# A recurrent block and an FP4 gated block on one core: the loop over two chunks written out as sixteen chunks

## The reference

```python
xn = layernorm(x)
# attention branch
a  = causal_dwconv3(rmsnorm(xn)) @ pw.T + b + xn          # x1
hidden, gate = split(rmsnorm(a) @ gru_w.T)                # 256 + 256
h[t] = sigmoid(-gate[t]) * h[t-1] + sigmoid(gate[t]) * g(hidden[t])
b_ = h + a                                                # x2
s  = gelu(rmsnorm(b_) @ w1.T + b1) @ w2.T + b2 + b_       # 256 -> 1024 -> 256
# gated branch, inputs and weights rounded to FP4 in blocks of 16
q  = fp4(xn)
hid = silu(q @ fp4(w_gate).T) * (q @ fp4(w_up).T)         # 256 -> 704
f  = fp4(hid) @ fp4(w_down).T                             # 704 -> 256
out = x + s * silu(f)
```

## Time and profile before

| | us |
|---|---|
| median of 3 runs | 1191.91 |
| lowest and highest run | 1191.78 and 1193.99 |
| profiled execution, its own time | 1193.24 |
| its span, first to last instruction | 1191.2 |
| its mean granted TensorE clock | 0.979 of full speed |

### The profile page before, as it was taken

The page is one execution under the profiler, slowest core; times in us unless marked ns, Lnnn a source line. Parts: engine busy times, 40 slices in busy tenths (PEclk is TensorE's granted clock), DMA queues, the critical chain, the costliest instruction groups (busy, mean ns, idle before and its releaser), DMA issues.

```text
span 1191.2 us, 18158 instructions
## 1 busy us (share of the span) xinstructions
PE 1102.8 (93%) x6306; PEld 969.6 (81%) x6306; DVE 865.2 (73%) x1638; ACT 549.9 (46%) x887; POOL 143.1 (12%) x122
## 2 busy tenths in 40 slices
PE   3467999999999999999999999999999999999998
PEld 2355988879898888988888798987889888888987
DVE  5777686868868586885868678686777858777655
ACT  3235454454545455453545444454444434544441
POOL 3010020101102010110201011020201101020010
PEclk9587999999999999999999999999999999999999
DMA  6000000010101001010010101001010100100000
GB/s 225 1 0 18 19 27 28 1 55 1 36 18 34 22 1 53 1 36 20 1 53 1 54 1 36 19 1 55 1 36 17 36 19 1 53 1 18 18 19 18
DMA packets 29355, 31.46 MB, mean 26 GB/s; under 512 B 1120, under 2 KB 28512, under 8 KB 29280
## 3 DMA queue, kind: packets, MB, share of 16 engines
q1 hardware_dynamic: 20000, 21.04, 5.6%
q10 hardware_dynamic: 9280, 9.26, 2.4%
HBM read 21.90 MB, written 8.39 MB: 25 GB/s over the span
## 4 chain that ended last, share of the span: by engine, by line
PE 76%; DVE 15%; issue 4%; ACT 4%; DMA 0%; POOL 0%; DVEq 0%; ACTq 0%; POOLq 0%
PE gu_ps L855 39%; PE w_ps L855 26%; PE w_ps L918 3%; DVE hqt_lo L471 2%; DVE x L506 2%; DVE hq L393 2%; DVE q_amax L367 2%; PE gu_ps L901 1%; PE w_ps L862 1%; ACT hqt_hi L732 1%; PE w_ps L873 1%; PE gu_ps L862 1%; DVE q_y L379 1%; PE w_ps L901 1%; DVE cand L504 1%
## 5 line engine op out<-in xcount | busy, mean ns | idle before, releaser
L855 PE MATMUL w_ps<-w,act 128*128 128x256 f32 x960 | 217.1, 379 | 0.0
L455 DVE TENSOR_TENSOR hid<-sl,gu_ps 128x352 f32<-128x352 f32 x128 | 65.7, 514 | 189.2 <-ACT sl L721 189.1
L855 PEld LDWEIGHTS w_ps<-w,act 128*128 128x128 f32 x960 | 177.7, 190 | 21.7
L855 PE MATMUL gu_ps<-gu_hi,xq_hi 128*128 128x352 f32 x512 | 170.1, 332 | 10.5 <-issue 9.5
L855 PE MATMUL gu_ps<-gu_lo,xq_hi 128*128 128x352 f32 x512 | 166.7, 326 | 1.7 <-issue 1.6
L855 PE MATMUL gu_ps<-gu_hi,xq_lo 128*128 128x352 f32 x512 | 166.4, 325 | 0.0
L855 PE MATMUL w_ps<-dn_hi,hqt_hi 128*128 128x256 f32 x384 | 119.6, 312 | 8.6 <-DVE hqt_lo L471 8.6
L721 ACT ACTIVATE sl<-gu_ps 128x352 f32<-128x352 f32 x128 | 59.4, 464 | 133.9 <-PE gu_ps L855 133.5
L327 POOL TENSOR_TENSOR inv_rms<-ss_row,neg_half 128x4 f32<-128x4 f32 x32 | 40.6, 1270 | 596.3 <-DVE ss_row L481 596.3
L759 ACT ACTIVATE act<-gu_ps,cols 128x512 f32<-128x512 f32 x128 | 86.5, 688 | 54.7 <-PE gu_ps L855 54.6
L855 PE MATMUL gu_ps<-xs_hi,w_hi 128*128 128x512 f32 x256 | 106.2, 415 | 3.1 <-DVE xs_lo L495 3.1
(11 more groups left out here) (115 smaller groups left out, 2199.4 us busy)
## 6 DMA issues: line engine op xcount, KB each, us to landing
x_in<-x_dram SPq DMA_DIRECT2D x16, 512.0 KB, 4.5
x_res<-x_dram ACTq DMA_DIRECT2D x16, 512.0 KB, 3.5
out_dram<-o SPq DMA_DIRECT2D x15, 512.0 KB, 3.2
act<-w_t_dram SPq DMA_DIRECT2D x1, 1024.0 KB, 13.3
w<-w_t_dram SPq DMA_DIRECT2D x1, 1024.0 KB, 15.6
act<-w_down_dram SPq DMA_DIRECT2D x1, 704.0 KB, 10.3
hid<-w_gate_dram SPq DMA_DIRECT2D x1, 640.0 KB, 5.6
hid<-w_up_dram SPq DMA_DIRECT2D x1, 640.0 KB, 9.2
```

The lines of the kernel that those rows point to most:

```text
L455: V.tensor_tensor(hid[:, t, h * HALF:(h + 1) * HALF], sl[:, h, :], gu_ps[:, h, 1, 0:HALF], ALU.mult).then_inc(hid_ready, 1)
L855: done = M.matmul(psum, l, r, start=first and i == 0, stop=last and i == len(terms) - 1)
```

## The change

The loop in `over_chunks` is replaced by a loop of the program that writes the kernel, so that the calls of `body` for chunks 1 to 14 follow each other as plain instructions. The chunk's number is now a constant in each, and the counts that are waited for with it.

```diff
         def over_chunks(engine, body):
 
             body(0, 0, False, True)
-            with engine.Fori(0, (B - 2) // 2) as i:
-                body(i * 2 + 1, 1, True, True)
-                body(i * 2 + 2, 0, True, True)
+            for c in range(1, B - 1):
+                body(c, c % 2, True, True)
             return body(B - 1, 1, True, False)
```

## The result

The changed kernel takes **1176.85 us**, the median of 4 runs (1176.37 to 1178.61), where the kernel before, run beside it, took 1192.95 us (4 runs, 1191.78 to 1194.89). The ratio is 0.9866 with a 95% interval of 0.9847 to 0.9885. The prediction was 1178.0 us, in a range from 1175.3 to 1181.4.

The account below looks back on a forecast made before the run. The prediction took TensorE to bound the kernel: 1193.24 us profiled less 15.2 for six branches back, or median 1191.91 less 13.9, gives 1178.0 us, with straight code and register instructions at 0. Range 1175.3 to 1181.4 us.

Parts of the forecast that it names:

- The bound and the six branches: Chunks 1 to 14: TensorE bounds the time, and its six branches back cost 15.2 us together, all on the path.
- long distances: Times between successive chunks' 18-matmul down-product pieces that hold a branch back, such as 70.85 and 72.32 us; expected to become 68.7.
- plain distances: Times between successive chunks' 18-matmul down-product pieces without a branch back between them; mean 68.73 us.
- The register instructions: Loop register work that vanishes from four engines; priced at 0 by comparing chunk 14 with chunk 15.
- Differences instead of idle time: Branch cost taken as 977.45 less 14 plain chunk distances, 15.2 us, rather than idle time alone, about 9.6 us.
- the one spell of low clock: Behind the branch at 541.55, TensorE ran briefly at 1.2 instead of 2.4 GHz; 1.3 us, within the 15.2.
- The clock: No low-clock spell expected without a branch stop; the rival had one or two, 1179 to 1181 us, chance 0.08.
- From the sum to the median: Whole kernel: 1193.24 - 15.2 for the profiled execution, 1191.91 - (15.2 - 1.3) for the median, both 1178.0 us.
- Straight code fetches without stalls: Written-out chunks 1 to 14: new program text takes a looped chunk's time, within 0.03 us; cost taken 0.
- The first pass: The loop's first pass, all code new, 8 and 4 packets, had the shortest distance; evidence that new text costs nothing.
- The slower rival: VectorE and ScalarE fetch in every chunk, stopping VectorE about 1.6 us each; 22.4 us more, 1200.4 us, chance 0.03.
- the rival of no gain: TensorE keeps its loop body and the six stops have another cause, so they stay; 1191.9 us, chance 0.03.

Follow-up runs that it names:

- passes of four: TensorE loops over four chunks in three passes, the rest written out, against the changed kernel: 1182.87 us, ratio 0.9909.
- The last experiment: Against the changed kernel, VectorE, ScalarE and GpSimd loop over four chunks in three passes, TensorE stays written out: 1185.88 us, ratio 0.9938.
- 200, announced: The kernel before, TensorE's loop head placed at instruction 200 of a block and the branch back announced at each pass's head: 1178.41 us, ratio 0.988.
- sixteen in a small loop: Changed kernel with one six-matmul group issued three times a chunk, two as passes of a small TensorE loop: 1206.06 us; all written out 1206.15.

## Why the prediction was right

**The bound and the six branches: right.** All six long distances became 68.70, and the gain within the chunks is 15.66 us where the sum had 15.2. The missing 0.4 us is that plain distances shrank from 68.73 to 68.70, which the prediction took as zero. The register instructions are a candidate: with TensorE alone written out the fourteen chunks take 962.22 us, with all four 961.79. But it doesn't add up engine by engine, since with TensorE alone in the loop the plain distances are 68.76 to 68.84 us, longer than with all four in it. Where these hundredths come from stays open.

**Differences instead of idle time: right.** The idle time at the six branches alone would have given 9.6 us. One sign was off for the same reason: TensorE's busy time was to stay near 1101 us and fell to 1098.3, as more of each branch's cost lay in slower matmuls than the one spell of low clock accounts for.

**The clock: right in this kernel.** No spell of the lower level appears in the chunks, and the profiled window in the middle has 1.00. One profile before and one after don't prove that it can't. How long TensorE stood still doesn't decide it either: a spell followed stops of 1.77 us (the kernel before) and 1.94 (TensorE alone in the loop), and none followed 1.94 and 1.80 (passes of four) or 1.93 and 1.87 (head at 200).

**From the sum to the median: partly luck.** The prediction took 15.2 us from the profiled execution and only 13.9 from the median, as the median run might have had no spell. The profiled executions came out 16.2 us apart and the medians, run side by side, 16.1. So 13.9 was 2.2 us too small. Only 1.15 of it shows in the number, as the median before, run beside the changed kernel, was 1.04 us higher than the one that the forecast started from. That the median run lacked a spell is not shown.

**Straight code fetches without stalls: right.** The first pass was a sound witness. The packets came out at 51 and 27, within the forecasts of 50 to 60 and 20 to 32.

**The slower rival: it didn't occur, but its mechanism exists.** Plain text is fetched ahead, so 27 packets cost nothing. The last experiment shows that fetches on VectorE and ScalarE that are not ahead cost some 4.7 us where they coincide, more than the 1.6 us that the rival borrowed from TensorE. The price was set too low for that place.

**A reason that was wrong, though no number hung on it.** Under the rival of no gain, the prediction took the 9 packets of a pass to disagree with a rule of the Trainium skill ("Runtime: NRT & Kernel Launch", section Instruction fetch mechanics) that gives TensorE room for 2048 instructions. The runs agree with the rule as far as they go: bodies of one chunk and of two, some 800 and 1,610 instructions, are kept once they touch few enough blocks. What the size alone doesn't tell is that room is counted in blocks, by where the head lies, with the block fetched ahead on top. "TensorE's loop body is not kept" was true of this loop at this address, not of a loop over two chunks. The other rule of the Trainium skill that was doubted there, a compare-and-branch of about 108 ns in "Advanced Engine Details and Errata", section Control Flow Timing, is not contradicted: sixteen of them were too cheap to measure, though no row shows the 108 ns itself. The rule that the prediction did find in agreement, from that same section of the Trainium skill on instruction fetch, that a taken branch waits when its target is outside a window of two pages, fits the stops of the kernel before but not the later runs: with the head at 0 or 128 each branch goes back over six blocks or more, and no branch had a stop of 0.3 us or brought a packet.

**What of it is shown.** That the stop is the fetch of pushed-out text is shown by one body at two addresses. That exactly 8 blocks are kept is not shown: between 128 and 200 no place was tried, and the block fetched ahead as the ninth is inferred from the 9 packets. The four loops over two chunks whose body was kept have ratios of 0.9888 (announced, and head at 0), 0.9878 (head at 128) and 0.988 (200, announced), the changed kernel 0.9866, and the intervals overlap: of the 1.3% nearly all is to be had without writing anything out. The changed kernel has the lowest ratio of all that ran, if not clear of the others.

## What to carry to other kernels

A constant gap with the releaser "issue" once in a pass, and an instruction queue whose packets grow with the passes, point to a loop whose text is pushed out and fetched again; compare the packets of the first pass with those of the second. Writing the loop out cured it here, and so did a shorter body, a head placed so that the body touches fewer blocks (0 or 128 of 256 here), or an announced branch, each at a small part of the text. When a loop is made longer on an engine with slack, look at what that engine does first after its branch, who waits for it, and whether it issues a large load just ahead of the branch, before calling the branch free.

## What the hardware showed that I had not expected

- The same loop costs 14 us more or less by where it begins: head at instruction 200 of a block 1192.46 us and 68 packets, at 128 1178.52 us and 13. Any edit ahead of a loop can thus move the time by 1.2% without touching the loop.
- Thirteen branches back on the bounding engine, to text that is kept, left the kernel at 1177.98 us, and sixteen in a small loop moved 1206.15 to 1206.06.
- A stop for a fetch was 1.5 to 1.9 us of idle time on TensorE, 2.1 on VectorE and 4.9 on ScalarE. TensorE may have worked off queued matmuls meanwhile, and ScalarE's fetch may have waited behind its own load, which was not tested.
